# Poolings with stationary softmax weights and moving tokens, and key logits that take four output groups in turn

## The reference

```python
scale = 1.0 / np.sqrt(DH)
queries = x_q @ Wq + bq
q_w = softmax((queries @ Wqa + bqa) * scale, axis=-2).transpose(0, 2, 1)
pooled_q = jnp.einsum('nhl,nhld->nhd', q_w, _sep(queries))      # weighted mean over the tokens, per head
keys = x_kv @ Wk + bk
keys_queries = keys * pooled_q.reshape(N, 1, C)
k_w = softmax((keys_queries @ Wka + bka) * scale, axis=-2).transpose(0, 2, 1)
pooled_k = jnp.einsum('nhl,nhld->nhd', k_w, _sep(keys))
values = _sep(x_kv @ Wv + bv)
keys_values = _grp(values * pooled_k[:, :, None, :]) @ Wt + bt
out = _grp(_sep(keys_values) + _sep(queries)) @ Wp + bp
```

## Time and profile before

| | |
|---|---|
| median of 3 runs | 763.26 us (760.21 to 765.3) |
| span of the profiled execution | 865.4 us |
| TensorE matmul busy in it | 578.2 us (67%) |
| TensorE weight load busy | 451.0 us (52%) |
| VectorE busy | 418.2 us (48%) |
| ScalarE busy | 234.8 us (27%) |
| GpSimd busy | 340.6 us (39%) |
| mean granted TensorE clock | 0.797 |

### The profile page before, as it was taken

How to read it: one execution, slowest core, us unless ns; L and a number is a source line. 1 busy time by engine, 2 the same in 40 slices (tenths; PEclk the granted TensorE clock), 3 DMA queues, 4 the chain that set the end, 5 groups by cost and what they waited for, 6 DMA issues and landing times.

```text
span 865.4 us, 17483 instructions
## 1 busy us (share of the span) xinstructions
PE 578.2 (67%) x5468; PEld 451.0 (52%) x5469; DVE 418.2 (48%) x1454; ACT 234.8 (27%) x411; POOL 340.6 (39%) x424
## 2 busy tenths in 40 slices
PE   2588765233598988882798887667572047999970
PEld 1256544011387877772454665545351026888860
DVE  5774777663232323234884668266173811222225
ACT  1220011220043343343521554233241111222220
POOL 6122046476045454555400000612515665555660
PEclk9786957655799999997699997567555578999995
DMA  7801001131222222232754353232204112222219
GB/s 209 225 25 37 13 26 40 35 125 53 72 71 67 62 65 62 69 119 68 231 172 125 97 151 105 75 99 50 57 8 141 37 49 76 69 69 73 75 43 291
DMA packets 73195, 76.52 MB, mean 88 GB/s; under 512 B 12984, under 2 KB 61368, under 8 KB 73064
## 3 DMA queue, kind: packets, MB, share of 16 engines
q1 hardware_dynamic: 58504, 50.98, 21.3%
q0 software_dynamic: 10224, 22.40, 8.4%
q10 hardware_dynamic: 4400, 2.26, 0.9%
HBM read 46.15 MB, written 29.34 MB: 87 GB/s over the span
## 4 chain that ended last, share of the span: by engine, by line
PE 35%; DVE 20%; issue 16%; another core or an unknown queue 11%; POOL 8%; DMA 4%; ACT 3%; SPq 2%; DVEq 1%; ACTq 0%; POOLq 0%
PE PS L758 31%; POOL ys L528 5%; DMA work<-ys 2%; DVE XN L1340 2%; DVE work L1314 2%; POOL xs L517 2%; DVE stats L1319 2%; DVE work L1729 2%; DVE X L1314 1%; DVE rtmp L1314 1%; POOL turn L526 1%; PE PS L939 1%; PE PS L1089 1%; DVE mv L1322 1%
## 5 line engine op out<-in xcount | busy, mean ns | idle before, releaser
L517 POOL DMA_INDIRECT xs<-pack,adr_i x80 | 79.1, 988 | 235.3 <-ACT pack L1164 154.2
L758 PE MATMUL PS<-w,work 128*128 x1152 | 145.7, 280 | 14.0 <-ACT work L1212 6.5
L528 POOL DMA_INDIRECT ys<-work x144 | 141.0, 979 | 34.1 <-issue 34.1
L758 PEld LDWEIGHTS PS<-w,work 128*128 128x128 f32 x1152 | 135.5, 193 | 25.0 <-issue 24.0
L758 PE MATMUL PS<-work,w1h 128*128 128x256 f16 x576 | 101.9, 278 | 22.7 <-issue 14.1
L1212 ACT ACTIVATE work<-PS,b 128x256 f32<-128x256 f32 x160 | 62.6, 477 | 117.1 <-PE PS L758 93.1
L1314 DVE TENSOR_TENSOR work<-PS,work 128x256 f32<-128x256 f32 (+3 forms) x82 | 33.0, 404 | 121.7 <-issue 75.5
L758 PE MATMUL PS<-work 97*64 97x256 f16 (+5 forms) x608 | 75.5, 318 | 17.2 <-DVE work L1446 10.9
L758 PE MATMUL PS<-work,w1l 128*128 128x256 f16 x288 | 79.9, 278 | 0.6 <-issue 0.6
L758 PEld LDWEIGHTS PS<-work 97*64 97x64 f16 (+2 forms) x608 | 57.8, 165 | 28.4 <-DVE work L1446 13.5
L758 PEld LDWEIGHTS PS<-work,w1h 128*128 x576 | 53.5, 99 | 31.7 <-issue 25.8
(11 more groups left out here) (261 smaller groups left out, 877.3 us busy)
## 6 DMA issues: line engine op xcount, KB each, us to landing
work<-xs SPq DMA_DIRECT2D x132, 65.0 KB
work<-ys SPq DMA_DIRECT2D x12, 512.0 KB, 5.9
k_parts<-work SPq DMA_DIRECT2D x24, 128.0 KB
w<-k_parts SPq DMA_DIRECT2D x8, 384.0 KB
work<-k_parts SPq DMA_DIRECT2D x32, 96.0 KB
work<-q_parts SPq DMA_DIRECT2D x8, 384.0 KB
work<-q_parts SPq DMA_DIRECT2D x32, 96.0 KB
ys<-work POOLq DMA_INDIRECT x144
```

Source lines behind the costliest of these rows:

```text
L517: g.indirect_dma_start(xs[l], bass.IndirectOffsetOnAxis(adr_i[:, k, T:T + 1], 0), pack_of(l, c)[:, s, k, :].bitcast(U32), None)\
L528: g.indirect_dma_start(ys[l], bass.IndirectOffsetOnAxis(xin[:, q, u, :].bitcast(U32)[:, D:D + 1], 0), yrow[:, q, u, :], None).then_inc(ff[ ...
L758: return t.matmul(o, lhsT, rhs, start=start, stop=stop, skip_group_check=True)
```

## The change

Each pooling's 16 matmuls swap their operands: `w2blk` of a tile (32 columns) is stationary and the tile's 128 token features move. The output is 32 rows by 128 columns, written to the 32-partition groups j = 0 to 3 in turn. The result has features along the free dimension, so ScalarE copies it to `prod` and four transposes bring it back to features on the partitions, in the same PSUM bank. The key logits keep their shape and go through the four groups in turn instead of eight times in the same one.

```diff
-                for T in range(a * NT // 2, (a + 1) * NT // 2):
-                    ins = mm(PF[:, 1024 + T * 32:1024 + (T + 1) * 32], src[:, T, :],
-                             w2blk[:, T, :, :].rearrange("p b h -> p (b h)"))
+                for i in range(NT // 8):
+                    for j in range(4):
+                        T = a * NT // 2 + 4 * i + j
+                        ins = mm(PS[32 * j:32 * j + 32, 2 + a, i * D:(i + 1) * D],
+                                 w2blk[:, T, :, :].rearrange("p b h -> p (b h)"), src[:, T, :])
+                ins.then_inc(soft["rows"], 1)
+                pe.wait_ge(soft["rows_sb"], 2 * r + a + 1)
+                for i in range(NT // 8):
+                    o = slice(a * 512 + i * P, a * 512 + (i + 1) * P)
+                    ins = t.transpose(PS[:, 2 + a, i * P:(i + 1) * P], prod[:, o], ident[:])
                 ins.then_inc(soft["pooled"], 1)
...
             def key_logits(a):
                 pe.wait_ge(gsem["sb"], a + 1)
-                for b in range(a * NB // 2, (a + 1) * NB // 2):
-                    c, bb = b // CB, b % CB
-                    j = 32 * (c % 4)
-                    ins = mm(PS[j:j + 32, 6 + a, bb * SEQ:(bb + 1) * SEQ], g32[:, b, :], ctT[:, b * SEQ:(b + 1) * SEQ])
+                for bb in range(CB):
+                    for j in range(4):
+                        b = (4 * a + j) * CB + bb
+                        ins = mm(PS[32 * j:32 * j + 32, 6 + a, bb * SEQ:(bb + 1) * SEQ], g32[:, b, :],
+                                 ctT[:, b * SEQ:(b + 1) * SEQ])
...
                 elif step == "pooled":
+                    act.wait_ge(soft["rows"], 2 * m + n + 1)
+                    if m == 1:
+                        act.wait_ge(soft["head_prod"], n + 1)
+                    a.activation(prod[:, half], PS[:, 2 + n, :], ACT.Copy).then_inc(soft["rows_sb"], 1)
                     act.wait_ge(soft["pooled"], 2 * m + n + 1)
                     a.activation(xp[:, half], PS[:, 2 + n, :], ACT.Copy).then_inc(soft["pooled_sb"], 1)
```

More of the change, by code:

```diff
@@ L273, in build @@
         c_ps, c_done = sem("c_ps"), sem("c_done")
-        soft = {k: sem(f"soft_{k}") for k in ("logits", "shifted", "exp", "weights", "wT", "blocks", "pooled",
-                                              "pooled_sb", "projected", "head_prod")}
+        soft = {k: sem(f"soft_{k}") for k in ("logits", "shifted", "exp", "weights", "wT", "blocks", "rows",
+                                              "rows_sb", "pooled", "pooled_sb", "projected", "head_prod")}
         gsem = {k: sem(f"g_{k}") for k in ("moving", "ps", "sb")}
```

## The result

The changed kernel has a median of 754.8 us against 763.5 us, a ratio of 0.990 with a 95% interval of 0.986 to 0.994. In a later comparison with more runs it was 0.994 (0.991 to 0.998). Both are inside the range; the forecast of 756.7 us is a ratio of 0.991.

The account below looks back on a forecast made before the run. TensorE was taken to bound the kernel up to about 90 us, then VectorE, GpSimd's scatters and queues. 5.1 us before 90 us plus about 1.5 from the fourth pooling gave 763.26 - 6.6 = 756.7 us, range 752.5 to 762.

Parts of the forecast that it names:

- Poolings and key logits: TensorE's new matmuls: a pooling 1.1 us at full clock or 2.2 at low, key logits 1.1 or 2.3 us.
- The added piece: Two copies, transposes and four hand-overs between pooling and projection: 2.1 us at full clock, 2.5 at low.
- First pooling: At 46.5 us: projection starts 1.3 us earlier, but the XN tiles' due time limits the gain to 1.1 us.
- First key logits: At 61.36 us, low clock: 2.3 for 4.53 us, less 0.4 for dearer transposes, a gain of 1.8 us.
- Second pooling: At 67.43 us: the row copy waits for the key softmax's exponential in ScalarE's queue, a loss of 0.8 us.
- Third pooling: At 75.75 us, low clock: start to projection 4.7 instead of 7.73 us, a gain of 3.0 us.
- Sum at 90 us: Gains up to 90 us: 1.1 + 1.8 - 0.8 + 3.0 = 5.1 us.
- two rivals of 0.20 and 0.13: Clock stays low longer: 4.1 us back, 760.8 us (0.20). Clock stays up: some 4.5 us more gain, 752 us (0.13).
- Fourth pooling: At 114.09 us: 3.0 us less on TensorE, at most 2.2 us going on through VectorE; about 1.5 taken for timed runs.
- The sign of a low clock beyond 90 us: A granted clock of 0.50 beyond 90 us would show the prediction wrong.
- No overlap between the groups: Rival, chance 0.09: 16 matmuls take 3.1 us at full clock or 6.9 at low; 5.2 us slower, 768.5 us.
- The scatters absorbing the fourth pooling: Case inside the forecast's 0.58: GpSimd's scatters absorb the fourth pooling's gain, leaving only 5.1 us, 758.2 us.

Follow-up runs that it names:

- row_copy_first: Changed kernel with ScalarE's row copy of the second pooling put ahead of the key softmax's exponential; ratio 0.982, repeated at 0.984.
- pool4_old: Changed kernel with the fourth pooling alone in its old form; ratio 0.997.
- after_again: Changed kernel, unedited, run and profiled a second time; ratio 0.994 to the kernel before.
- split_later: Kernel of row_copy_first with one expert's weight split moved from ahead of the first routing to behind the first addresses; ratio 0.991.
- kl_only: Kernel before the change with only the key logits taking the four groups in turn; ratio 0.999.
- serial: Changed kernel with each pooling's 16 matmuls writing one group four times before going to the next; ratios 0.992 and 0.987 in two runs.
- before_again: Kernel before the change, unedited, profiled a second time; span 760.4 us.

## Why the prediction was right, and where it was not

**Poolings and key logits.** The time per pooling, 1.1 or 2.2 us, measured 1.08 and 1.94. The prediction took it from a weighing that "differs in width alone"; that row has 18 stationary columns and the poolings have 32, which made no difference that these numbers show. The added piece was right: pooling start to projection 4.46 us in the third pooling, forecast 4.7.

**First pooling, 1.1 us.** Right: the key logits start 1.04 us earlier. TensorE waits 1.17 us for XN before chunk 6, as the due time said.

**First key logits, 1.8 us.** Too small; it was 2.74. I kept the low clock that this place had before. There the clock fell at 60.9 us, ahead of their start at 61.36; here it fell at 61.2 us, and the key logits had started at 60.32 and were nearly done. The sentence that the softmax weights "are no bound" was wrong: the transposes behind them waited for just these weights (0.17 to 0.33 us idle at TensorE in the timelines), so more could not come.

**Second pooling, a loss of 0.8.** It was 0.67, and the mechanism is shown by row_copy_first.

**Third pooling, 3.0 us.** It was 3.27 at the low clock.

**Sum at 90 us.** 5.1 forecast, 6.45 between the two first profiles, 7.9 between the two second ones (87.95 to 80.08), which both had a better clock; crosswise it is 4.35 and 9.97. The term I mis-sized is the clock. I had it as two rivals of 0.20 and 0.13 for the whole of the kernel. It is neither: it differs between executions of one program and moves attended chunk 0 by 2.1 us before and 3.5 us after the change.

**Fourth pooling, 2.2 us through the profile, 1.5 taken.** VectorE's wait is gone, and 1.26 us arrive at the last scatter, by pool4_old against after_again (1.0 us between the means of all profiles). So the size was about right up to there, and the reason is the one the prediction named: without the idle time in GpSimd's waits, part of the 2.2 us is lost. Behind it 0.04 us are left at the first store, in an execution whose clock was low just then, and no timed run shows the rest.

**The total.** The medians differ by 8.7 us in the first comparison and by 5.1 us in the later one (763.4 and 758.3), the forecast was 6.6. The stages are right as told above, but that the total came out this close is also luck: the clock alone moves the first part by more than it is off.

**The sign of a low clock beyond 90 us.** It came, though it was named as a sign of being wrong. The kernel before had full clock from 88.2 to 108.7 us; the changed kernel's first profile is low from 95.4 to 98.8 and from 102.2 us, after_again from 89.5 to 96.3. It cost nothing up to the first scatter, which starts 28.5 us behind attended chunk 0 in every profile but split_later's.

**Rivals.** No overlap between the groups: its mechanism does not happen, and when it was forced, its prices (3.1 and 6.9 us) were too high by 0.6 and 2.4 us, and a 5 us slower kernel did not follow. I scaled the low-clock price from a 512-column product with a 128-column stationary operand; the direct row is 0.28 us a matmul (4.50 for 16), not 0.43. The scatters absorbing the fourth pooling: they absorbed about 0.9 of its 2.2 us.

## What to carry to other kernels

When an fp32 matmul has a wide stationary and a narrow moving operand, swap them: the 128-column weight loads were the price here (7.04 us a pooling, 4.50 swapped and 1.94 with groups in turn, all at the low clock), and the swap paid even with a copy and four transposes to bring the result back. A saving on TensorE can be lost to the clock of what stands behind it: kl_only lost 1.1 of its 2.2 us in the next pooling, and a slower order of groups was as fast (serial). Take a second profile when the span of the first lies 100 us above the timed runs, and judge an edit of a few microseconds by marks in the trace, with the clock of both executions beside each mark: pool4_old looked worth nothing at the first store because its partner's clock was low there.

## What the hardware showed that I had not expected

The granted clock of the same program over the same 20 us was 0.51 in one execution and full from 72 us on in the next. The four profiles in which TensorE had more to do there, by the serial order or the idle matmuls, all had full clock at the third pooling; of the seven with both operands swapped and groups in turn but no fillers, four had it. The times of the rise say the same: in three of the first four the clock was back at 67.2 to 68.2 us and in the fourth it had not fallen, in the six with both parts, groups in turn and no fillers it was back at 71.8 to 82.6 us. That is suggestive, not proven.

The clock doesn't follow what TensorE does at the moment. It came back while TensorE was idle (64.3 us in kl_only, 75.4 us in before_again) and fell in the midst of a busy pooling (67.7 and 78.9 us).

One group after the other, 16 fp32 matmuls of 32 stationary and 128 moving columns take 2.46 us at full clock, in four groups in turn 1.08, a factor of 2.3. For 32 with 64 moving columns it is 3.18 against 1.10, a factor of 2.9.
